# Partial sums, merge, queries and value pieces at other places of a chunk, and a feed-forward part in two halves

## What is computed

```python
x = x + _layernorm(_L0_attn_ref(_layernorm(x), Wq, bq, Wk, bk, Wv, bv, Wo, bo))
x = x + _layernorm(_L0_ffn_ref(_layernorm(x), U1, V1, b1, U2, V2, b2))

# attention
q = einsum('bsd,dhk->bshk', x, Wq) + bq          # k and v likewise
attn = softmax(einsum('bqhd,bkhd->bhqk', q / sqrt(64), k))
out = einsum('bqhd,hdm->bqm', einsum('bhqk,bkhd->bqhd', attn, v), Wo) + bo

# feed-forward, rank 32, 512 hidden columns
H = gelu((x @ U1) @ V1 + b1)
return (H @ U2) @ V2 + b2
```

## Time and profile before

| | us |
|---|---|
| median of 3 runs (lowest, highest) | 2488.88 (2484.93, 2494.09) |
| the profiled execution, its own time | 2491.32 |
| its span, first to last instruction | 2489.5 |
| PE busy | 2407.4 (97%) |
| ACT busy | 2171.3 (87%) |
| DVE busy | 2067.8 (83%) |
| POOL busy | 2018.3 (81%) |
| share of PE, of DVE in the chain that ended last | 88%, 8% |

### The profile page before, as it was taken

How to read it: one execution, slowest core, us unless ns; L and a number is a source line. 1 busy time by engine, 2 the same in 40 slices (tenths; PEclk the granted TensorE clock), 3 DMA queues, 4 the chain that set the end, 5 groups by cost and what they waited for, 6 DMA issues and landing times.

```text
span 2489.5 us, 44216 instructions
## 1 busy us (share of the span) xinstructions
PE 2407.4 (97%) x15724; PEld 1195.9 (48%) x15724; DVE 2067.8 (83%) x3231; ACT 2171.3 (87%) x2491; POOL 2018.3 (81%) x1117
## 2 busy tenths in 40 slices
PE   6999999999999999999999999999999999998885
PEld 3455454544454454454455455445445545544332
DVE  7788888888888888888888888888888888888877
ACT  5989889888888988988889988998898898887884
POOL 4888888888888888888888888888888888887673
PEclk8999999999999999999999999999999999999887
DMA  1000000000010000000010000100000000000011
GB/s 49 28 14 27 27 18 28 27 27 14 27 32 18 23 27 27 19 27 27 14 32 27 20 21 27 32 14 27 27 20 27 27 27 22 27 27 22 26 35 30
DMA packets 60773, 63.13 MB, mean 25 GB/s; under 512 B 25900, under 2 KB 44204, under 8 KB 60556
## 3 DMA queue, kind: packets, MB, share of 16 engines
...
...
## 4 chain that ended last, share of the span: by engine, by line
PE 88%; DVE 8%; issue 2%; ACT 1%; DMA 1%; POOL 0%; POOLq 0%; SPq 0%; ACTq 0%; DVEq 0%
PE o_ps L401 34%; PE spare_ps L358 13%; PE score_ps L380 10%; PE score_ps L383 9%; PE score_ps L386 9%; PE spare_ps L344 3%; DVE max_part L739 3%; PE spare_ps L431 3%; PE spare_ps L335 3%; PE spare_ps L326 2%; DVE part_sum L770 1%; PE spare_ps L413 1%; PE spare_ps L365 1%; DVE z_sb L716 1%; DVE ln_stats L705 1%
## 5 line engine op out<-in xcount | busy, mean ns | idle before, releaser
L929 POOL TENSOR_TENSOR total<-total,probs 128x832 f32<-128x832 f32 x896 | 1766.1, 1971 | 345.4 <-ACT probs L592 276.4
L739 DVE TENSOR_REDUCE max_part<-spare_ps 128x1 f32<-128x512 f32 x2027 | 1304.3, 686 | 332.7 <-PE spare_ps L358 315.1
L592 ACT ACTIVATE probs<-score_ps 128x1024 f32<-128x1024 f32 x1024 | 993.1, 1023 | 233.2 <-PE score_ps L386 231.1
L582 ACT ACTIVATE score_ps<-m_all 128x1024 f32<-128x1024 f32 x1024 | 1010.1, 1028 | 7.1 <-DMA m_all<-m_scratch 7.1
L401 PE MATMUL o_ps<-probs,v_sb 128*64 128x512 f32 x4096 | 995.6, 600 | 0.0
L358 PE MATMUL spare_ps<-k_hi,q_hi 64*128 64x512 f32 x2027 | 464.3, 451 | 27.4 <-DVE max_part L739 20.0
L401 PEld LDWEIGHTS o_ps<-probs,v_sb 128*64 128x64 f32 x4096 | 305.1, 137 | 385.9 <-issue 268.2
L380 PE MATMUL score_ps<-q_hi,k_hi 64*128 64x512 f32 x2048 | 421.5, 407 | 7.4 <-ACT score_ps L582 7.4
L358 PEld LDWEIGHTS spare_ps<-k_hi,q_hi 64*128 64x128 f32 x2027 | 196.4, 184 | 460.4 <-issue 285.8
L386 PE MATMUL score_ps<-q_hi,k_lo 64*128 64x512 f32 x2048 | 406.3, 392 | 0.0
L383 PE MATMUL score_ps<-q_lo,k_hi 64*128 64x512 f32 x2048 | 405.9, 392 | 0.0
...
## 6 DMA issues: line engine op xcount, KB each, us to landing
...
m_scratch<-max_rows SPq DMA_DIRECT2D x64, 4.0 KB
denom_col<-denom SPq DMA_DIRECT2D x63, 4.0 KB
denom_scratch<-denom_col SPq DMA_DIRECT2D x63, 4.0 KB, 1.4
```

Of the source, the lines that this page charges most:

```text
L582: nc.scalar.activation(score_ps[st % 2][:], m_all[:, G % 2], ACT.Copy).then_inc(s["seed_done"], 1)
L592: nc.scalar.activation(probs[:, st % RING], score_ps[st % 2][:], ACT.Exp, scale=SCALE).then_inc(s["exp_done"], 1)
L739: nc.vector.reduce_max(max_part[:, G % 2, h, qt, kc:kc + 1], bank[max_bank(n, h)], AX.X).then_inc(s["max_done"], 1)
L929: nc.gpsimd.tensor_tensor(others(total[:, G % 2]), so_far, others(probs[:, st % RING]), ALU.add).then_inc(s["sum_done"], 1)
```

## The change

It does three things.

1. **Places in a chunk.** A partial sum is taken at the end of doubles 3, 5, 6 and 1 of the next chunk (PART_AT) and no longer at 2, 4, 6 and 0 of the next. The merge moves from double 1 to 2, the denominators from 2 to 3, their DMA from 3 to 4, the queries from 3 to 2. The value pieces are counted over all 16 tiles and may cross a group of four: still 11 pieces, five of two tiles, six of one.
2. **First half of the feed-forward part.** Six groups run from double 471 on, with bases 471, 477, 484, 491, 498, 505, up to the low-rank product (k_lo and k_hi of batch row 0, free by then, hold it). The first normalise is ACT's (`act_t1`), the addition of x and the second normalise are POOL's (`pool_x1`, `pool_xn`).
3. **Second half.** Everything from the hidden product on, for all groups, follows the last exponential, in an order written out by hand, with the four score banks for the hidden product and two tiles for its gelu. Groups 6 and 7 run whole there. The last norm is POOL's for groups 0 to 3 and DVE's for 4 to 7.

```diff
-V_AT = {(0, 6): (0, 0, 2), (1, 0): (0, 2, 2), (1, 6): (1, 0, 2), (2, 0): (1, 2, 1), (2, 4): (1, 3, 1), (2, 6): (2, 0, 1),
-        (2, 7): (2, 1, 2), (3, 0): (2, 3, 1), (3, 4): (3, 0, 1), (3, 6): (3, 1, 1), (3, 7): (3, 2, 2)}
-MERGE_AT, L_AT, DENOM_OUT_AT, RECIP_AT, NEG_MAX_AT, NORM_AT = 1, 2, 3, 5, 4, 7
-Q_AT, M_AT = 3, 5
+V_AT = {(0, 6): (0, 2), (1, 0): (2, 1), (1, 6): (3, 2), (2, 0): (5, 1), (2, 4): (6, 2), (2, 6): (8, 2), (2, 7): (10, 1),
+        (3, 0): (11, 1), (3, 4): (12, 1), (3, 6): (13, 2), (3, 7): (15, 1)}
+MERGE_AT, L_AT, DENOM_OUT_AT, RECIP_AT, NEG_MAX_AT, NORM_AT = 2, 3, 4, 5, 4, 7
+Q_AT, M_AT = 2, 5
+PART_AT = {3: 0, 5: 1, 6: 2, 1: -1}
...
-FFN_BASE = [488, 492, 496, 500, 504, 508, 512, 515]
+FFN_BASE = [471, 477, 484, 491, 498, 505]
+ST1, R1, T1, X1, ST2, XN, XT, P_AT, LOW = 0, 1, 2, 3, 5, 6, 8, 9, 10
+FIN = 4
...
+            for k in range(FF // P):
+                me.user[H_BANKS[k]] = "exp", STEPS - 2 + k // 2
+            me.values(STEPS - 2)
+            me.values(STEPS - 1)
+            me.hidden(0)
+            me.xn_columns(5)
+            me.hidden(1)
+            me.last_denominators(CHUNKS - 1)
+            me.second_rank(0)
...
-                if d % 2 == 0 and n:
-                    dve_part(dve, n // 2 - 1)
+                if d in PART_AT and (G or PART_AT[d] >= 0):
+                    dve_part(dve, G * (T // GROUP) + PART_AT[d])
...
+            dve_out(dve, 6)
+            dve_z(dve, 7)
+            dve_out(dve, 7)
...
+        def act_t1(act, g):
+            act.wait_ge(f["f_rs1"], g + 1)
+            for t in range(TC):
+                nc.scalar.activation(y_acc[:, g * TC + t, :], y_acc[:, g * TC + t, :], ACT.Identity,
+                                     bias=ln_shift[:, g % 2, t:t + 1], scale=ln_rstd[:, g % 2, t:t + 1]).then_inc(f["f_t1"], 1)
...
+        def pool_x1(pool, g):
+            pool.wait_ge(f["f_t1"], TC * (g + 1))
+            pool.wait_ge(g_in[g % 2], 16 * (g // 2 + 1))
+            nc.gpsimd.tensor_tensor(x1_tile(g), x1_tile(g), xg[:, g % 2], ALU.add).then_inc(f["f_x1"], 1)
+
+        def pool_normalise(tiles, outs, slot, out_sem):
+            for t in range(TC):
+                nc.gpsimd.tensor_scalar(outs[t], tiles[t], ln_mv[:, slot, t, 0:1], ln_rstd[:, slot, t:t + 1],
+                                        ALU.subtract, ALU.mult).then_inc(out_sem, 1)
...
+            pool_r1(pool, 6)
+            pool_x1(pool, 6)
+            pool_xn(pool, 6)
+            pool_out(pool, 0)
+            pool_r1(pool, 7)
+            pool_out(pool, 1)
+            inverse_deviation(pool, 3, f["f_mv2"], f["f_ep2"], f["f_rs2"], 7)
+            pool_out(pool, 2)
+            pool_out(pool, 3)
+            for g in range(FIN, NG):
+                pool_r3(pool, g)
```

568 lines of the change are left out of this document (331 added, 237 removed).

## The result

| | before | changed |
|---|---|---|
| median of 4 runs, us | 2489.73 | 2463.59 (2463.04 to 2465.16) |
| ratio, 95% interval | | 0.990, 0.9884 to 0.9916 |
| span of the profiled execution | 2489.5 | 2461.0 |
| a unit in the middle (unit 12) | 145.48 | 144.01 |
| start of the last unit | 2235.17 | 2216.75 |

The kernel is faster by 26.1 us, 1.0%, where 53.7 were forecast. The time is inside the range of the prediction (2405 to 2470), but 27.6 above the 2436 that it settled on, over twice the 12 us that it took a measurement to tell, so each term has to be looked at.

The account below looks back on a forecast made before the run. The prediction took PE to bound the repeating part, while in the last unit engines wait for each other. Its terms, -27 + 2 - 41.7 + 11.4 = -55.3, lead from 2491.3 to 2436 us, range 2405 to 2470.

Parts of the forecast that it names:

- places, 15 units: Fifteen units before the last: moved places cut PE's waits from 3.3 to 1.5 us, 1.8 per unit, 27 in all.
- doubles 471 to 479: Doubles before the last unit: statistics on DVE and POOL's lag cost 2 us more.
- last unit: Last unit, up to the start of the last double: 155 us instead of 196.74, 41.7 less; bounds 141 and 172.
- behind the last double: From the start of the last double to the end: 69 us instead of 57.59, 11.4 more; bounds 58 and 85.
- I take 0.37, nearest to the two POOL rows: Feed-forward part: one 128x128 normalisation on POOL was estimated at 0.37 us from POOL's rows at 832 and 512 columns.
- far bound of 1.1: Highest price considered for one 128x128 normalisation on POOL, 1.1 us, what DVE's took beside POOL.
- second rival: Feed-forward part: POOL slower than its rows say, 44 normalisations at 1.1 instead of 0.37, 32 us more, 2465; chance 10%.
- double 6 as before, 4.6 of 4.35: Double 6 of each chunk: DVE's load stays 4.6 us against the double's 4.35, an overload under 0.3.
- the double after keys or queries, eight times a unit: Repeating part: where PE's 0.08 us wait for ACT's seeding was said to stay, moving from double 4 to 3.
- about 0.1 stays in double 7 behind it: Double 7 of each chunk: a wait of about 0.1 us per chunk remains behind double 6's sum.
- The last unit as POOL's: POOL needs 4.9 us a double where PE needs 4.3 to 4.5, so it lags and bounds the last unit.
- signs named: What would show the prediction right, such as a 143.7 us unit, POOL over 90% busy, last unit 155, rest 69.

Follow-up runs that it names:

- e1_places: The kernel before with only the change's table of places in a chunk, old feed-forward part kept: 2466.51 us, ratio 0.9899.
- e16_m_late: The changed kernel with ACT's 0.25 us copy of the maxima's row (double 5) put behind the two seeds instead of ahead: 2458.16 us, ratio 0.9873.
- e11_price: The changed kernel with every normalisation on POOL cut to 4 of its 128 columns, the rest left out: 2445.34 us.
- e3_part7: The changed kernel with the third partial sum of a chunk in double 7 instead of 6: 2462.18 us, ratio 0.9886.
- e10_xn_act: The changed kernel with the second normalisation (to xn) of groups 0 to 6 on ACT instead of POOL: 2447.97 us, ratio 0.9835.

## Why the prediction was wrong, by its own steps

| term of the sum | forecast | measured | missing |
|---|---|---|---|
| places, 15 units | -27 | -21.4 (`e1_places`, start of the last unit) | 5.6 |
| doubles 471 to 479 | +2 | +2.9 | 0.9 |
| last unit | -41.7 | -33.1 | 8.6 |
| behind the last double | +11.4 | +23.1 | 11.7 |
| sum | -55.3 | -28.5 | 26.8 |

The first measured value is `e1_places` against before, the second the change against `e1_places` at the same point; the others are the spans' own windows. The sum is that of the profiled executions; by the medians the change has 26.1.

- **The step that failed** is "I take 0.37, nearest to the two POOL rows". A normalisation on POOL took 0.80. The reasoning went by columns and by the number of tensors read, and called 0.45 an upper bound by size; the runs show 3.4 ns a column, not 2.16, and a price of operations and scalars on top. The step is in both the last-unit term and that of the end: with 0.38 in place of 0.80 (`e11_price`) these come to 156.5 and 70.9, 1.5 and 1.9 from the forecast. So 7.1 + 9.7 = 16.8 of the 26.8 are this one number. The granted clock rose with it (0.96 to 0.98 in the last unit, 0.76 to 0.82 behind it); what of the 16.8 is the clock's wasn't separated. The 3.4 left in these two terms are near the scatter of the last unit. The far bound of 1.1 was the better end, and the second rival named the mechanism. That its time, 2465, is so near is luck: at 0.80 the rival's own rate (29 us for 0.73) gives 17, and 2453; the rest came from the other terms.
- The Trainium skill's rule that was weighed there (GPSIMD Engine Reference, section Engine selection: with one input about line rate) would have made it 0.3, an estimate. The trace has 0.80 on POOL and 0.34 for the same instruction on DVE; the measurement decides, and the rule doesn't hold for this form, two operations with scalars from a column.
- **The places** were right in mechanism: no wait is left between second maximum pair and output projection, double 5 has only the seeding's, double 3 has the seeding's 0.08 in place of double 4, no exponential waits for a partial sum. What failed is "double 6 as before, 4.6 of 4.35", which looked at DVE alone, and the list of ACT's seeding waits, "the double after keys or queries, eight times a unit": a copy of 0.25 ahead of the seeds does it too, and PE's wait for DVE in double 5, which the change removes, had hidden it. It cost 0.4 per unit, some 5 us in all (`e16_m_late`). Units 1 to 14 gained 1.47 each in `e1_places` where 1.8 were forecast, 4.7 in all, and with the copy moved they gain the 1.8. That unit 0 gained only 0.3 and not 1.8 was not foreseen, and why stays open; 0.5 the other way comes from before the first double. These are the 5.6.
- **Sums in double 6**: "about 0.1 stays in double 7 behind it" was right, 0.08, and `e3_part7` took it away.
- **The last unit as POOL's**: right. POOL was busy 92% of it (93% from double 484 on), and taking its normalisations to ACT shortened it by 12.0 (`e10_xn_act`).
- **The end**: four outputs at the end 5.4 apart, where 5.1 were forecast. The fifth output's normalisation started 60 behind the start of the last double where 49 were forecast, behind POOL's four outputs, each 0.23 + 1.04 + 3.14 + 1.27, 5.9 with gaps.
- Of the signs named, these were there: one table load ahead of the gelus, POOL above 90%, no exponential waiting for a partial sum, outputs some 5 apart. These were not: a unit of 143.7 (144.0), a normalisation of 0.3 to 0.45 (0.80), a last unit of 155 (163.6), a rest of 69 (80.6).
